# Causal mask of a row-maximum pass: 28 spare contraction rows in place of 384 bf16 mask matmuls

## Time and profile before

| | us |
|---|---|
| median of 3 runs | 898.99 (898.91 to 899.19) |
| span of the profiled execution, first to last instruction | 895.5 |
| TensorE matmuls busy | 832.9 |
| VectorE busy | 673.4 |
| ScalarE busy | 414.4 |
| GpSimd busy | 241.8 |
| attention stage in the profile | 93.6 to about 470 |

### The profile page before, as it was taken

The page is one execution under the profiler, slowest core; times in us unless marked ns, Lnnn a source line. Parts: engine busy times, 40 slices in busy tenths (PEclk is TensorE's granted clock), DMA queues, the critical chain, the costliest instruction groups (busy, mean ns, idle before and its releaser), DMA issues. The chain is left out here.

```text
span 895.5 us, 12571 instructions
## 1 busy us (share of the span) xinstructions
PE 832.9 (93%) x4509; PEld 569.0 (64%) x4509; DVE 673.4 (75%) x1100; ACT 414.4 (46%) x682; POOL 241.8 (27%) x309
## 2 busy tenths in 40 slices
PE   3799899999999999999988999999997899999983
PEld 2687544445545555455446878878786788887772
DVE  6888878886688668866663556566746999599977
ACT  2224166665566556655762454554454432242321
POOL 5000134543344344534442101111000000026406
PEclk9899999999999999999998999999997999999997
DMA  5630302222222222221344453512102325115762
GB/s 148 226 120 21 73 18 82 73 65 75 67 79 71 67 70 79 73 68 62 117 138 142 152 168 109 182 48 73 45 12 88 126 86 172 59 37 173 227 234 94
DMA packets 53886, 89.93 MB, mean 100 GB/s; under 512 B 10288, under 2 KB 18496, under 8 KB 52416
## 3 DMA queue, kind: packets, MB, share of 16 engines
q1 hardware_dynamic: 53824, 89.13, 31.8%
HBM read 47.69 MB, written 28.31 MB: 85 GB/s over the span
## 5 line engine op out<-in xcount | busy, mean ns | idle before, releaser
L805 DVE TENSOR_REDUCE rowmax<-ps 128x1 f32<-128x384 f32 (+3 forms) x384 | 217.8, 594 | 74.3 <-PE ps L855 72.4
L731 ACT ACTIVATE probs<-ps 128x512 f32<-128x512 f32 (+1 forms) x352 | 191.1, 559 | 134.0 <-PE ps L867 132.9
L867 PE MATMUL ps<-stack,ks 128*128 128x512 f32 (+1 forms) x352 | 157.6, 453 | 2.5 <-DMA stack<-ml 2.0
L853 PE MATMUL ps<-km,stack 128*128 128x512 f32 (+2 forms) x384 | 150.1, 400 | 2.8 <-PEq L163 1.9
L713 POOL TENSOR_SCALAR_AFFINE_SELECT probs<-probs 128x512 f32<-128x512 f32 x128 | 79.8, 634 | 126.5 <-ACT probs L731 126.4
L853 PEld LDWEIGHTS ps<-km,stack 128*128 128x128 f32 x384 | 73.9, 192 | 59.0 <-DVE rowmax L805 41.4
L1588 PE MATMUL ps<-big_h 128*128 128x512 f32 x256 | 100.9, 394 | 9.2 <-DVE big_l L1513 9.2
L1260 PE MATMUL ps<-big_h,w1h 128*128 128x512 f32 x256 | 105.5, 412 | 1.4 <-DVE w1l L1131 1.4
L1262 PE MATMUL ps<-big_h,w1l 128*128 128x512 f32 x256 | 102.1, 399 | 0.0
L1261 PE MATMUL ps<-big_l,w1h 128*128 128x512 f32 x256 | 101.5, 397 | 0.0
L1590 PE MATMUL ps<-big_h,big_l 128*128 128x512 f32 x256 | 100.5, 392 | 0.0
(11 more groups left out here) (190 smaller groups left out, 1366.8 us busy)
## 6 DMA issues: line engine op xcount, KB each, us to landing
stack<-big_h SPq DMA_DIRECT2D x128, 64.0 KB, 2.0
projected_rows<-w2t_scratch SPq DMA_DIRECT2D x32, 256.0 KB, 2.7
h_scratch<-hs SPq DMA_DIRECT2D x7, 1024.0 KB, 4.4
hload<-h_scratch SPq DMA_DIRECT2D x14, 512.0 KB, 5.1
xn_scratch<-xa SPq DMA_DIRECT2D x4, 1024.0 KB, 4.5
stack<-big_l SPq DMA_DIRECT2D x64, 64.0 KB, 2.0
xi<-xn_scratch SPq DMA_DIRECT2D x16, 256.0 KB, 2.7
xe_scratch<-xm SPq DMA_DIRECT2D x16, 256.0 KB, 2.3
```

Source lines behind the costliest of these rows:

```text
L731: nc.scalar.activation(probs[:, o:o + nh * w], ps[:, STB[n % NST], 0:nh * w], ACT.Exp).then_inc(s_exp, 1)
L805: nc.vector.tensor_reduce(dst, src, AX_X, ALU.max).then_inc(s_red, 1)
L853: nc.tensor.matmul(dst, stack[u % 3][:, hp, P * qt:P * (qt + 1)], km[:, u // KT, p0:p0 + npar, 0:w], start=True, stop=False)
L867: ins = nc.tensor.matmul(ps[:, STB[n % NST], 0:nh * w].rearrange("p (h q) -> p h q", h=nh), ks[:, u // KT, p, P * kt:P * (kt + 1)], stack[ ...
```

## The change

The stack's partitions 100 to 127 and the same partitions of `km` no longer hold zeros but a causal mask as a product. Each of the 28 rows covers a run of 5 query positions. In row r the query side has 1, 2^-25, ... 2^-100 at the 5 positions of its run and 0 elsewhere; the key side has 0 ahead of the run, -1, -2^25, ... -2^100 along it and -2^125 behind it. The product is -2^25 or less for every key later than the query, -1 for the query's own key, and of size 2^-25 or less for earlier keys of the run. So the matmul that multiplies queries and keys over all 128 rows masks by itself, and the mask matmul L855 is gone.

Keys of earlier 128-blocks need no mask, and are multiplied over 96 rows only; keys of the query's own block over all 128. A matmul of before that had both kinds becomes two. Per head pair there are now 8 fp32r matmuls with 256, 256 + 256, 512, 256 + 256, 384 and 384 columns, in place of 6 fp32r ones (256, 512, 384, 384, 512, 512) and 6 bf16 mask ones (256, 256, 128, 128, 128, 128). The fourth piece holds the own blocks of query tiles 2 and 3, so their maxima come in two parts, and VectorE joins them once per unit behind its last reduction; `maxima` waits for that (`s_rm`).

`later_q` and `later_k` are built by GpSimd in the preparation, one memset and 7 selects each; `fill_spare` copies `later_q` into the stack, and `later_k` is copied into `km` for each sequence and parity. `ks` is computed from `km` before that copy, and keeps its zeros.

```diff
-NEG = -1e30
+SPARE, RUN, STEP = 100, 5, 2.0 ** 25
...
+        later_q = sa("later_q", [P, P])
+
+        def fill_spare(i):
+            spare = slice(6 * HD, P)
+            return nc.gpsimd.tensor_copy(stack[i][spare, :, :].rearrange("r h (j k) -> r (h j) k", k=P),
+                                         later_q[spare, :].rearrange("r (o k) -> r o k", o=1)
+                                         .broadcast_to([P - 6 * HD, NPAIR * QT, P]))
...
-                step(nc.gpsimd.memset(hidden_mask[:, :, :], 0.0))
-                nc.gpsimd.affine_select(out=hidden_mask[:, :, :], in_=hidden_mask[:, :, :], compare_op=ALU.is_ge,
-                                        fill=NEG, base=0, pattern=[[0, 2], [-1, P]],
-                                        channel_multiplier=1).then_inc(s_const, 1)
-                nc.gpsimd.memset(stack[0][6 * HD:P, :, :].bitcast(F32), 0.0).then_inc(s_z, 1)
+                def steps_along(tile, values):
+                    step(nc.gpsimd.memset(tile[:, :], 0.0))
+                    for t, v in enumerate(values):
+                        step(nc.gpsimd.affine_select(out=tile[:, :], in_=tile[:, :], compare_op=ALU.is_ge, fill=v,
+                                                     base=t - 1 - RUN * SPARE, pattern=[[-1, P]],
+                                                     channel_multiplier=RUN))
+                    step(nc.gpsimd.affine_select(out=tile[:, :], in_=tile[:, :], compare_op=ALU.is_ge, fill=0.0,
+                                                 base=-SPARE, pattern=[[0, P]], channel_multiplier=1))
+                steps_along(later_q, [STEP ** -s for s in range(RUN)] + [0.0])
+                steps_along(later_k, [-STEP ** t for t in range(RUN + 1)])
+                fill_spare(0).then_inc(s_z, 1)
+                for g in range(B):
+                    pool.wait_ge(s_paf, a_at[("kv", g, 0)] + 1)
+                    for p in range(2):
+                        nc.gpsimd.tensor_copy(km[6 * HD:P, g, p, :].rearrange("r (j k) -> r j k", k=P),
+                                              later_k[6 * HD:P, :].rearrange("r (o k) -> r o k", o=1)
+                                              .broadcast_to([P - 6 * HD, QT, P])).then_inc(s_kz, 1)
...
-        PIECES = [(0, 0, 2), (1, 0, 2), (2, 0, 1), (2, 1, 1), (3, 0, 1), (3, 1, 1)]
+        PIECES = [[(0, True, 0, 2)], [(1, False, 0, 2), (1, True, 0, 2)], [(2, False, 0, 2)],
+                  [(2, True, 0, 2), (3, True, 0, 2)], [(3, False, 0, 1)], [(3, False, 1, 1)]]
...
                 for i in (1, 2):
-                    nc.gpsimd.memset(stack[i][6 * HD:P, :, :].bitcast(F32), 0.0).then_inc(s_z, 1)
+                    fill_spare(i).then_inc(s_z, 1)
...
+                        bank, mine = ps[:, MAXB[g % NMAX], :], rowmax[:, u % 2, :, :]
+                        if m == 3:
+                            src = bank.rearrange("p (s a k) -> p s a k", s=2, a=2)
+                            dst = mine[:, QT:QT + 2, :].rearrange("p s (a h) -> p s a h", a=2)[:, :, :, hp]
...
                         nc.vector.tensor_reduce(dst, src, AX_X, ALU.max).then_inc(s_red, 1)
+                        if c == CH - 1:
+                            dve.wait_ge(s_red, g + 1)
+                            nc.vector.tensor_tensor(mine[:, 2:QT, :], mine[:, 2:QT, :], mine[:, QT:QT + 2, :],
+                                                    ALU.max).then_inc(s_rm, 1)
...
-                    nc.tensor.matmul(dst, stack[u % 3][:, hp, P * qt:P * (qt + 1)],
-                                     km[:, u // KT, p0:p0 + npar, 0:w], start=True, stop=False)
-                    nc.tensor.matmul(dst[:, :, w - P:w], ident_b[:, :], hidden_mask[:, 0:npar, :],
-                                     start=False, stop=True).then_inc(s_max, 1)
+                    for qt, own, p0, npar in PIECES[m]:
+                        rows = slice(0, P if own else 6 * HD)
+                        keys = slice(P * qt, P * qt + P) if own else slice(0, P * qt)
...
+                        last = nc.tensor.matmul(dst, stack[u % 3][rows, hp, P * qt:P * (qt + 1)],
+                                                km[rows, u // KT, p0:p0 + npar, keys], start=True, stop=True)
+                    last.then_inc(s_max, 1)
...
                 def maxima(u):
-                    pe.wait_ge(s_red, CH * (u + 1))
+                    pe.wait_ge(s_rm, u + 1)
```

More of the change, by code:

```diff
@@ L111, in block_layernorm_attention_ffn @@
         b1_in = sp_("b1_in", [FT, P])
+        later_k = sp_("later_k", [P, P])
         s_x0 = [sem(f"x_tile{j}_loaded") for j in range(QT)]
@@ L130, in block_layernorm_attention_ffn @@
         s_magc = sem("column_magic_ready")
-        s_z = sem("stacks_zeroed")
+        s_z = sem("spare_rows_filled")
+        s_kz = sem("later_keys_marked")
         s_sq = [[sem(f"stack{i}_queries{hp}") for hp in range(NPAIR)] for i in range(3)]
@@ L237, in _ @@
                 pool.wait_ge(s_const, 1)
[L238 to L247 removed]
+                nc.gpsimd.tensor_copy(ident_b[:, :], ident[:, :]).then_inc(s_const, 1)
+                def steps_along(tile, values):
[9 more added lines that the diff above has]
+                fill_spare(0).then_inc(s_z, 1)
+                pool.wait_ge(s_z, 1)
+                for g in range(B):
[4 more added lines that the diff above has]
+                                              .broadcast_to([P - 6 * HD, QT, P])).then_inc(s_kz, 1)
+                pool.wait_ge(s_kz, 2 * B)
             IDENT_READY, COLS_READY, ALL_READY = 1, 2, 3
@@ L455, in block_layernorm_attention_ffn @@
         P_OFF = [NPAIR * sum(T - P * j for j in range(k)) for k in range(QT)]
-        rowmax = sa("rowmax", [P, 2, QT, HPF])
+        rowmax = sa("rowmax", [P, 2, QT + 2, HPF])
         mh = sa("mh", [HPF, T], F32R)
@@ L484, in block_layernorm_attention_ffn @@
         s_red = sem("max_reduced")
+        s_rm = sem("row_maxima_whole")
         s_st = sem("scores_full")
@@ L802, in _ @@
                         dve.wait_ge(s_max, g + 1)
-                        src = ps[:, MAXB[g % NMAX], 0:npar * w].rearrange("p (a k) -> p a k", a=npar)
-                        dst = rowmax[:, u % 2, qt, :].rearrange("p (a h) -> p a h", a=2)[:, p0:p0 + npar, hp]
+                        bank, mine = ps[:, MAXB[g % NMAX], :], rowmax[:, u % 2, :, :]
+                        if m == 3:
+                            src = bank.rearrange("p (s a k) -> p s a k", s=2, a=2)
+                            dst = mine[:, QT:QT + 2, :].rearrange("p s (a h) -> p s a h", a=2)[:, :, :, hp]
+                        else:
+                            qt, _, p0, npar = PIECES[m][0]
+                            w = P * (qt + 1) if qt < 2 else P * qt
+                            src = bank[:, 0:npar * w].rearrange("p (a k) -> p a k", a=npar)
+                            dst = mine[:, qt, :].rearrange("p (a h) -> p a h", a=2)[:, p0:p0 + npar, hp]
                         nc.vector.tensor_reduce(dst, src, AX_X, ALU.max).then_inc(s_red, 1)
+                        if c == CH - 1:
+                            dve.wait_ge(s_red, g + 1)
+                            nc.vector.tensor_tensor(mine[:, 2:QT, :], mine[:, 2:QT, :], mine[:, QT:QT + 2, :],
+                                                    ALU.max).then_inc(s_rm, 1)
                     for at, part in NORM_AT.items():
@@ L851, in max_piece @@
                         pe.wait_ge(s_red, n - NMAX + 1)
-                    dst = ps[:, MAXB[n % NMAX], 0:npar * w].rearrange("p (a k) -> p a k", a=npar)
-                    nc.tensor.matmul(dst, stack[u % 3][:, hp, P * qt:P * (qt + 1)],
-                                     km[:, u // KT, p0:p0 + npar, 0:w], start=True, stop=False)
-                    nc.tensor.matmul(dst[:, :, w - P:w], ident_b[:, :], hidden_mask[:, 0:npar, :],
-                                     start=False, stop=True).then_inc(s_max, 1)
+                    bank, o = ps[:, MAXB[n % NMAX], :], 0
+                    for qt, own, p0, npar in PIECES[m]:
+                        rows = slice(0, P if own else 6 * HD)
+                        keys = slice(P * qt, P * qt + P) if own else slice(0, P * qt)
+                        w = keys.stop - keys.start
+                        if m == 1:
+                            dst = bank.rearrange("p (a k) -> p a k", a=2)[:, :, keys]
+                        else:
+                            dst = bank[:, o:o + npar * w].rearrange("p (a k) -> p a k", a=npar)
+                        o += npar * w
+                        last = nc.tensor.matmul(dst, stack[u % 3][rows, hp, P * qt:P * (qt + 1)],
+                                                km[rows, u // KT, p0:p0 + npar, keys], start=True, stop=True)
+                    last.then_inc(s_max, 1)
                 def scores(u, s):
```

5 lines of the change are left out of this document (removed).

## The result

| | before | changed |
|---|---|---|
| median of 4 runs each, us | 898.95 (897.57 to 899.19) | 873.07 (872.7 to 875.71) |
| ratio, 95% interval | | 0.9717 [0.9702, 0.9732] |
| span of the profiled execution | 895.5 | 874.0 |

The profiled execution took 875.71, the longest of the four. Run again later as e0, the changed kernel took 870.46 (869.57 to 874.77), ratio 0.9683 [0.9645, 0.9721], with a span of 869.2. The forecast was 869.5. One profiled execution in what follows, that of e4, ran at a lower granted clock than all others (0.745 on average, 996.75 us) and enters no comparison.

What follows compares the result with a forecast made beforehand. TensorE was taken to bound the attention stage, with the maxima's chain level in over half the units. Gains 1.5 + 13.2 + 16.2 less 0.8, 0.2 and 0.5 made 29.4 us: 899.0 to 869.5, range 856 to 884.

Steps and rivals of the forecast that it cites:

- Masks at 0.12 each, of either width: Row-maximum pass: each of 384 removed mask matmuls held TensorE 0.12 us, limited by the successor's weight load; 46.1 us gross.
- Splits nearly free, 96 rows free: Pass's matmuls: 128 more by splitting cost 0.01 to 0.02 us each, 2 us in all; 96-row operands cost nothing.
- The rival at 912: Slow side: 96-row matmuls change the array's shape at 0.10 us each way, 38 to 51 us lost; chance 0.08.
- The chain grows from 6.12 to 6.4: Time in us from the maxima's transposition to first scores, longer as both reductions ahead of the low part become 512 wide.
- 8 intervals with the stall, 1.65 less 0.1 each: Intervals where TensorE waits for the maxima in the stack: 13.2 us gained, 0.8 given back because DVE is nearly level.
- 6 intervals without it, 2.7 each: Projecting intervals without a stack wait: 24 masks save 2.88 us less 0.15 for splits, 16.2 us in all.
- Unit 0, 1.5 us: Interval of unit 0, 18.3 us: 17 masks behind its stall save 2.0, less 0.5 for chain and splits.
- First stretch, tail, preparation: First stretch bound by DVE, gain 0, loss 0.2 us; tail and FFN 0; GpSimd's preparation loses 0.5 us.
- DVE's idle falls by over 30: Sign of being right: DVE's idle time ahead of the reductions falls by more than 30 us.
- TensorE's idle for the stack 10 to 17: Sign of being right: TensorE's idle for the stack's DMA grows from 4.4 us to 10 to 17.
- Stall and chain hide elsewhere (856): Rival in the attention stage: all of the masks' time counts, 43 us gained, time 856; chance 0.12.
- L914 waits for the combine by over 0.3: Sign of being wrong: the maxima's transposition waits over 0.3 us for DVE's combine, priced at 0.25 per unit.

Runs made afterwards that it cites:

- e4: Changed kernel with a small 128-column bf16 matmul, into a bank nobody reads, behind each piece of the first unit; 874.44 us, ratio 0.972.
- e1: Changed kernel with a bf16 mask matmul of 128 columns put back behind each of the 384 pieces; 904.5 us, ratio 1.0048.
- e2: Changed kernel with a bf16 mask matmul of 256 columns put back behind each of the 384 pieces; 901.68 us, ratio 1.0015.
- e3: Changed kernel with all matmuls of the row-maximum pass over 128 rows, none over 96; 870.33 us, ratio 0.9671.
- e10: The kernel before, run once more without an edit; 900.48 us.
- e8: Changed kernel with the maxima's low part made one step earlier and the high part's DMA sent without waiting for it; 867.04 us, ratio 0.9642.
- e5: Changed kernel with VectorE making the low part of the maxima one step earlier; 869.13 us, ratio 0.966.
- e11: Kernel of e8 with the combine as a one-input tensor_reduce into its own tile, not a two-input tensor_tensor; 864.55 us, ratio 0.9622 against the kernel before.
- e6: Changed kernel with a unit's scores beginning 9 steps into the next unit, not 8; 878.35 us, ratio 0.9774.

## Why the prediction was right

The time was forecast at 869.5; measured were 873.07 and, with the kernels of the experiments, 870.46. The gain is TensorE's. By the intervals it is 26.0 of the 29.4 in the sum, so that 870.46 lies within 1 us of the forecast is in part luck. The terms below differ in both directions, and the first profile of before was a fast execution: wherever a time and its span are both on record they are 1.7 to 1.8 apart, which puts that profile at about 897.2, not at the median of 899.0.

- *Masks at 0.12 each, of either width.* Held: 0.12 in e1 and in e2, and 31 to 34 us came back with them. The reason given, the weight load of the successor, held too.
- *Splits nearly free, 96 rows free.* Held: e3; e1 and e2 leave 2.6 to 3.3 us for splits and all else from unit 1 on, where 2 was taken for the splits. The rival at 912 falls.
- *The chain grows from 6.12 to 6.4.* 6.40.
- *8 intervals with the stall, 1.65 less 0.1 each.* 1.37 on average, 10.95 in place of 12.4. GpSimd's selects now come late too: in e0 `probs` L741 held TensorE's L922 for 1.6 us in 7 times, a wait that the sum had left out. The intervals are 18.7 and 21.4 where 18.4 and 21.2 were forecast.
- *6 intervals without it, 2.7 each.* 15.17 in place of 16.2: the 25-us ones gave 2.76, the 22.5-us ones 2.4 and the last 2.06. I had priced the kinds alike.
- *Unit 0, 1.5 us.* This step failed: -0.52 against the first profile of before. The chain there grew by 0.86, not by about 0.3, and the low clock behind the first scores cost 1.7 more (4.0 x 0.43); 2.04 less 0.36, 0.50 and 1.7 is what was measured. I had taken over the granted clock of the earlier trace rows, 0.88 and 1.00, although the change takes a third of the matmuls out of the stretch ahead of that unit (48 to 31 in the windows above). Against e10's 19.83 unit 0 gained 1.0, so part of the term is that one execution of before was luckier.
- *First stretch, tail, preparation.* Unchanged within what varies between runs, the 0.5 for GpSimd included: it had its constants ready at 24 us, and the first matmul of the attention came at 93.25 to 94.4, against 93.68 and 93.99 in the two profiles of before. Of the 14 selects that I had put at 0.42 at most, 13 took 0.29 and one 2.16.
- *DVE's idle falls by over 30.* It fell by 26.2, since part of it turned from waiting for masks into waiting behind the stack's stall: in e8, where that stall is gone, VectorE's wait for TensorE is 38.8 in place of e0's 46.3. *TensorE's idle for the stack 10 to 17.* 22.5 in the row's own count, above the range. That count adds a weight load's wait to its matmul's, which I hadn't seen; its matmuls alone went from 2.0 to 9.6.
- *Stall and chain hide elsewhere (856).* Not as the change stands. But e5, e8 and e11 show that the mechanism was there to be had: 864.55, with four of the five short intervals at 17.83.
- *L914 waits for the combine by over 0.3.* It did, in 2 units of after, 0.9 us in sum and 0.6 at most. The prediction had named this as what would prove it wrong, and for those two units the price of 0.25 was. It missed that the combine can take 1.13 us beside GpSimd. It cost little, 1.2 us in the first profile, because only two units met it; in e0 no combine took over 0.52.

The gain left on the table is shown, not argued: 9 us of wait for the stack, of which 3.4 us came by sending the parts early (e8). Of the 2.5 more in e11, 1.7 came by taking the combine out of GpSimd's way. The new combine without the early parts wasn't tried.

## What to carry to other kernels

Price a short matmul by its effect on the starts behind it, not by its columns: ahead of 128 columns of fp32 weights, 128 and 256 columns cost the same 0.12 us here, and ahead of 8 columns 0.07 and 0.12. When work is taken off the busiest engine, look in the same pass for the return path that was hidden under it (here maxima, two halves, one queue), since it bounds the gain at once. A tiny instruction on that path wants one input from SBUF when GpSimd works beside it: a two-input `tensor_tensor` of 0.17 us took up to 1.29 (e6), a `tensor_reduce` for the same result 0.19 at most.

## What the runs showed of the hardware that was not expected

- The granted clock stayed at 1.2 GHz for 24 us (93.4 to 117.4, e0) while TensorE was shown busy for 11.55 of the 12 us from 100 to 112 (31 matmuls). In e10 it was back by 100 us and stayed at 2.4 to 112, with 48 matmuls that were shown busy for only 10.67. The busy share of a page doesn't tell which it will be.
- A us at 1.2 GHz cost 0.43 us of time in unit 0, from six profiles with 2.4 to 6.1 us of it.
- A bf16 matmul of 128 columns costs 0.12 us ahead of 128 columns of fp32 weights (load 0.20) and 0.07 ahead of 8 (load 0.09); one of 256 columns 0.12 in either place.
- A matmul over 96 rows costs at most 0.006 us more than one over 128 (0.17 and 0.18 for 384 columns by the starts), changes from one to the other included.
- A 16-element VectorE instruction took 0.17 to 1.29 us, its end set by a GpSimd instruction that began before it.
- A later start of the scores (e6) made the chain that it should cover longer, from 6.40 to 7.73.
